# Another order of the work inside a 128-row step of an adaLN cross-attention: DVE, ScalarE and GpSimd queues rearranged

## The reference

```python
def _ada_ln(x, c, W_ss, b_ss):
    h = (x - mu) / jnp.sqrt(var + EPS)
    scale, bias = jnp.split(silu(c) @ W_ss + b_ss, 2, axis=-1)
    return (1.0 + scale)[:, None, :] * h + bias[:, None, :]

xq  = _ada_ln(x_q,  t_vec, Wss_q,  bss_q)       # x_q  (16, 1024, 512)
xkv = _ada_ln(x_kv, t_vec, Wss_kv, bss_kv)      # x_kv (16, 64, 512)
q = (xq @ Wq + bq).reshape(B, Lq, 16, 32)
kv = (xkv @ Wkv + bkv).reshape(B, Lkv, 2, 16, 32)
scores = einsum('bqhd,bkhd->bhqk', q, k) / sqrt(32)
out = einsum('bhqk,bkhd->bqhd', softmax(scores), v).reshape(B, Lq, H)
return x_q + (out @ Wp + bp)
```

## Time and profile before

| what | us |
|---|---|
| median of 3 runs | 1309.93 (1308.97 to 1312.77) |
| the profiled execution's own time | 1311.49 |
| its span, first to last instruction | 1309.7 |
| busy: TensorE | 1165.9 (89%) |
| busy: VectorE | 1050.9 (80%) |
| busy: ScalarE | 872.3 (67%) |
| busy: GpSimd | 841.6 (64%) |

### The profile page before, as it was taken

The page is one execution under the profiler, slowest core; times in us unless marked ns, Lnnn a source line. Parts: engine busy times, 40 slices in busy tenths (PEclk is TensorE's granted clock), DMA queues, the critical chain, the costliest instruction groups (busy, mean ns, idle before and its releaser), DMA issues.

```text
span 1309.7 us, 32556 instructions
## 1 busy us (share of the span) xinstructions
PE 1165.9 (89%) x11072; PEld 693.8 (53%) x11072; DVE 1050.9 (80%) x1799; ACT 872.3 (67%) x1624; POOL 841.6 (64%) x941
## 2 busy tenths in 40 slices
PE   6897799898989998998989999898999999898997
PEld 2673455555555555554555555454555555454554
DVE  5746788888888888787888888787978888888896
ACT  2476667676776676676767677676766667676654
POOL 1544466767666776766666676766667675766744
PEclk9799899999999999999999999999999999999999
DMA  9010122222222222222222222222222222222222
GB/s 331 31 50 17 57 74 89 83 96 72 96 72 96 72 96 72 96 96 72 95 73 96 72 96 72 86 93 77 89 88 82 86 76 92 72 97 74 82 77 78
DMA packets 59871, 112.00 MB, mean 86 GB/s; under 512 B 6412, under 2 KB 6440, under 8 KB 59832
## 3 DMA queue, kind: packets, MB, share of 16 engines
q1 hardware_dynamic: 59832, 111.48, 25.0%
HBM read 77.90 MB, written 33.55 MB: 85 GB/s over the span
## 4 chain that ended last, share of the span: by engine, by line
PE 25%; issue 22%; POOL 18%; DVE 12%; ACT 10%; DMA 1%; POOLq 1%; ACTq 1%; DVEq 0%; SPq 0%
PE ps_q L1133 8%; PE ps_o L1201 7%; POOL xr L394 5%; POOL w_lo L432 4%; POOL xh L385 3%; PE ps_v L1116 3%; PE ps_t L1167 3%; DVE pr L876 3%; ACT junk L583 2%; POOL rstd L373 2%; DVE pr L896 2%; PE ps_s L1152 2%; PE ps_v L1186 2%; ACT xT_hi L510 2%; DVE mx L884 2%
## 5 line engine op out<-in xcount | busy, mean ns | idle before, releaser
L394 POOL TENSOR_TENSOR xr<-xr,bp_row 128x512 f32<-128x512 f32 x128 | 163.0, 1273 | 140.1 <-DMA xr<-in_x_dram 72.1
L603 ACT ACTIVATE pr<-pr,exp_scale 128x1024 f32<-128x1024 f32 x128 | 147.1, 1150 | 123.0 <-DVE pr L896 123.0
L558 ACT CAST pt_hi<-ps_t 128x512 f16<-128x512 f32 x256 | 138.0, 590 | 107.8 <-PE ps_t L1167 107.8
L846 DVE TENSOR_TENSOR xT_lo<-ps_v,xT_hi 128x512 f16<-128x512 f32 x120 | 83.0, 692 | 140.3 <-ACT xT_hi L510 140.3
L418 POOL TENSOR_TENSOR xr<-y,xr 128x512 f32<-128x512 f32 x128 | 162.5, 1270 | 25.5 <-POOL rstd L373 7.3
L425 POOL TENSOR_TENSOR half_den<-pr 128x512 f32<-128x512 f32 x128 | 162.9, 1272 | 22.8 <-DVE den L861 22.8
L432 POOL TENSOR_TENSOR w_lo<-w_tmp,w_hi 128x512 f16<-128x512 f32 x60 | 69.7, 1162 | 167.4 <-ACT w_hi L591 165.4
L884 DVE TENSOR_REDUCE mx<-ps_s 128x8 f32<-128x512 f32 x256 | 164.0, 683 | 12.4 <-PE ps_s L1152 12.4
L876 DVE SCALAR_TENSOR_TENSOR pr<-pr,ps_v 128x512 f32<-128x512 f32 x256 | 164.5, 684 | 4.4
L904 DVE TENSOR_TENSOR pt_lo<-ps_t,pt_hi 128x512 f16<-128x512 f32 x256 | 163.8, 682 | 0.2 <-ACT pt_hi L558 0.2
L896 DVE TENSOR_TENSOR pr<-ps_s,mx 128x512 f32<-128x512 f32 x256 | 163.8, 682 | 0.0
(11 more groups left out here) (162 smaller groups left out, 2348.9 us busy)
## 6 DMA issues: line engine op xcount, KB each, us to landing
x_in<-in_x_dram SPq DMA_DIRECT2D x128, 256.0 KB, 2.7
xr<-in_x_dram SPq DMA_DIRECT2D x128, 256.0 KB, 2.9
out_dram<-xr SPq DMA_DIRECT2D x128, 256.0 KB, 2.0
raw<-in_L_xcond_Wss_kv_dram SPq DMA_DIRECT2D x4, 512.0 KB, 5.4
cx<-in_ctx_dram SPq DMA_DIRECT2D x1, 2048.0 KB, 12.7
raw<-in_L_xcond_Wss_q_dram SPq DMA_DIRECT2D x4, 512.0 KB, 13.7
raw<-in_L_xcond_Wkv_dram SPq DMA_DIRECT2D x2, 1024.0 KB, 15.7
wq<-in_L_xcond_Wq_dram SPq DMA_DIRECT2D x1, 1024.0 KB, 17.0
```

Source lines behind the costliest of these rows:

```text
L394: pool.tensor_tensor(xr[:, s, :], xr[:, s, :], bp_row[:, :], ALU.add).then_inc(xr_ready, 1)
L558: act.copy(pt_hi[:, 4 * h:4 * h + 4, :], ps_t[:, h, :].rearrange("p (g n) -> p g n", g=4))\
L603: act.activation(pr[:, i % 2], pr[:, i % 2], ACT.Exp, scale=exp_scale[:, 0:1]).then_inc(exp_done, 1)
```

## The change

Only the order of calls inside three `step` functions changes, and with it which unit some calls handle. TensorE's and SP's code is untouched. No arithmetic is added or removed; ScalarE's prologue takes in the moments of one more unit (9), since `sum_rows` and `sum_squares` now run one unit further ahead, and `residual` handles unit i-4 where it handled i-2. The preparation of the query weights (`scaled_wq`, `scaled_wq_lo`) is one step later on GpSimd, `scaled_wq_hi` in the same step as before, and `values` moves from step 1 to step 2.

```diff
 # GpSimd
             def step(b, i):
-                half_sums(b, i - 1)
-                if 2 <= i <= 5:
-                    scaled_wq_lo(b + 1, i - 2)
-                if 1 <= i <= 4:
-                    scaled_wq(b + 1, i - 1)
                 await_rows(b, i + 9)
-                residual(b, i - 2)
+                residual(b, i - 4)
                 moments(b, i + 9)
                 await_moments(b, i + 9)
+                half_sums(b, i - 1)
+                normalise(b, i + 9)
                 add_rows(b, i - 4)
-                normalise(b, i + 9)
+                if 3 <= i <= 6:
+                    scaled_wq_lo(b + 1, i - 3)
+                if 2 <= i <= 5:
+                    scaled_wq(b + 1, i - 2)
 # ScalarE
                 turned_p(b, i - 2, 1)
-                sum_rows(b, i + 9)
+                if i == 2:
+                    values(b)
+                sum_rows(b, i + 10)
+                if i == 7:
+                    key_blocks(b + 1)
+                if i == 4:
+                    query_bias(b + 1)
+                query(b, i + 4)
+                turned_x(b, i + 8)
+                sum_squares(b, i + 10)
                 if exists(b, i):
...
                     wait(act, sub_done, 2 * upto(b, i))
                     act.activation(pr[:, i % 2], pr[:, i % 2], ACT.Exp, scale=exp_scale[:, 0:1]).then_inc(exp_done, 1)
-                turned_x(b, i + 8)
-                if i == 4:
-                    query_bias(b + 1)
-                query(b, i + 4)
-                sum_squares(b, i + 9)
+                if 2 <= i <= 5:
+                    scaled_wq_hi(b + 1, i - 2)
                 if isinstance(b, int) and b == 0 and i in (0, 1):
                     wp_high(i)
-                if 2 <= i <= 5:
-                    scaled_wq_hi(b + 1, i - 2)
-                if i == 1:
-                    values(b)
-                if i == 7:
-                    key_blocks(b + 1)
 # ScalarE, prologue
                         row_moments(8)
+                        row_moments(9)
 # VectorE; softmax_shift now takes the half h and does that half alone
             def step(b, i):
-                turned_o(b, i - 3)
                 score_max(b, i, 0)
                 score_max(b, i, 1)
-                softmax_shift(b, i)
+                turned_o(b, i - 3)
+                weight_sums(b, i - 1)
                 turned_p(b, i - 2, 0)
                 turned_p(b, i - 2, 1)
+                denominators(b, i - 1)
+                softmax_shift(b, i, 0)
+                softmax_shift(b, i, 1)
                 turned_x(b, i + 8)
-                weight_sums(b, i - 1)
-                denominators(b, i - 1)
+                query(b, i + 4)
                 if isinstance(b, int) and b == 0 and i in (0, 1):
                     wp_low(i)
                 normalise_p(b, i - 1)
-                query(b, i + 4)
```

More of the change, by code:

```diff
@@ L886, in score_max, with softmax_shift @@
                        .then_inc(mx_done, 1)
-            def softmax_shift(b, off):
+            def softmax_shift(b, off, h):
                 if not exists(b, off):
                     return
[L892 to L898, removed]
+                if h == 0:
+                    wait(dve, p_turned, 2 * unit(b, off - 1))
+                hs = slice(HALF * h, HALF * (h + 1))
+                wait(dve, mx_done, 2 * unit(b, off) + h + 1)
+                dve.tensor_tensor(pr[:, off % 2, hs, :], ps_s[:, h, :].rearrange("p (h l) -> p h l", l=LKV),
+                                  mx[:, hs].unsqueeze(2).to_broadcast([P, HALF, LKV]), ALU.subtract)\
+                   .then_inc(sub_done, 1)
             def turned_p(b, off, h):
```

## The result

The changed kernel takes 1184.82 us in the median of 4 runs (1183.3 to 1185.47), against 1311.06 for the kernel before in its own 4 runs; the ratio is 0.9036, with a 95% interval of 0.9018 to 0.9054. The forecast was 1184. The profiled execution took 1185.47, its span is 1183.7.

A forecast was written before the change was run, and what follows sets the result against it. The kernel was taken to be bound by TensorE's 8.21 us a step plus waits from a ring across engines. Gains of 119.4 + 6.2 = 125.6 us took the span from 1309.7 to 1184.1, the forecast median to 1184; range 1176 to 1226.

The forecast's parts named there:

- TensorE's floor: Steps from unit 8 to unit 120: each falls to TensorE's unwaited 8.21 us, 919.5 in all, a gain of 119.4 us.
- The ring through `w_hi`, `w_lo` and `xh`: ScalarE, GpSimd and TensorE, steps 2 to 5: w_lo's wait for w_hi delays xh; its 4.72 us in step 3 go.
- VectorE in time for `weigh` and the scores: VectorE's step: all five results TensorE wants are ready in time; least slack 0.57 us, xT_lo for weigh.
- The late exponential and `vb`, `kb` for nothing: ScalarE: vb in step 2 and kb in step 7, 1.33 us a pair, fill a wait; later exponential, 1.15, still in time.
- Start: Up to unit 8: first scores some 1.6 us later, unit 3 unchanged within 2 us, then five steps gain 6.2 us.
- The possible gain from a clock that stays up: TensorE's clock around 128 to 130 us: halving the wait could keep it up, some 3 us better, left for the range.
- End: The last eight units: already at their floors, no change taken.
- The half sums can start when the exponential ends, at 7.6: GpSimd: half sums start 0.6 us before the next step's scores and end 0.7 after; den wants them at 2.8.
- (a): TensorE: weigh waits for xT_lo, 0.3 us a step giving 1220 us, 0.6 giving 1256; chance 0.2 with cases between.
- (b): GpSimd's last third binds: w_hi waits for w_tmp if the full step is 8.7 us; 22 us, 1206; chance 0.1.
- (c): Slower: the late exponential closes a ring from turn_x to the next step's weigh; 30 us longer, 1340; chance 0.04.
- (d): The order makes no difference: a wait is for something else and returns at another instruction; 1310 us; chance 0.02.

The follow-up runs named there:

- less_pe: The changed kernel without the product of oT_hi with the low half of the output weights (4 of 12 matrix products of project_out); 1116.97 us, ratio 0.8528.
- w_last: The kernel before with only GpSimd's weight work (w_lo, w_tmp) moved from behind the half sums to the end of its step; 1273.64 us, ratio 0.9707.
- w_same_step: The changed kernel with GpSimd's weight quarters one step earlier, in the steps of the kernel before; 1326.26 us, ratio 1.0119.
- undo_dve: The changed kernel with VectorE's old order; 1226.54 us, ratio 0.9342.
- undo_dve_q: The changed kernel with VectorE's old order, but q_lo ahead of the sums; 1186.78 us, ratio 0.9035.
- exp_early: The changed kernel with ScalarE's exponential back in its early place, ahead of kb, q_hi and xT_hi; 1432.74 us, ratio 1.0909.
- start: The changed kernel with unit 9's row moments behind the last prologue halves on ScalarE, and VectorE normalising ahead of wp_low; 1181.24 us, ratio 0.9006.
- act_only: The kernel before with ScalarE's new order alone (late exponential, moments one unit further ahead); 1375.98 us, ratio 1.0488.
- undo_pool: The changed kernel with GpSimd's old order; 1443.73 us, ratio 1.0993.
- dve_only: The kernel before with VectorE's new order alone; 1772.54 us, ratio 1.351.
- pool_only: The kernel before with GpSimd's new order alone; 1972.43 us, ratio 1.5034.

## Why the prediction was right

The time (1184 against 1184.82) came out by its own steps, and not by errors that cancelled in the large terms: 119.75 us less between units 8 and 120 (119.4 reckoned) and 6.2 between units 3 and 8 (6.2). The small terms cancelled in part by luck, as said at the start below.

- *TensorE's floor.* Every step from unit 3 to unit 120 at 8.21: shown, 919.15 us for 112 steps against 919.5. That it is TensorE which sets it is shown by `less_pe`.
- *The ring through `w_hi`, `w_lo` and `xh`.* The 4.72 us wait is gone. I gave two reasons, that `w_lo` takes the `w_hi` of the step before and that it stands behind `xh`. For the ring of the kernel before the second is enough, as `w_last` shows, which has no wait at `w_lo` left. The first is needed in the new order, where `w_hi` stands behind the late exponential: `w_same_step`, without it, closes another ring.
- *VectorE in time for `weigh` and the scores.* Right; `xT_lo` has 0.82 us of slack where I had 0.57, since the reciprocal starts 0.16 us ahead of the subtraction and not 0.3, and `den` 0.60 ahead of `pt_lo` and not 0.7. `undo_dve` and `undo_dve_q` show that `q_lo` is the deadline that mattered.
- *The late exponential and `vb`, `kb` for nothing.* Right in the new order; `exp_early` shows what the early place costs there.
- *Start.* First scores 1.4 us later (1.6 reckoned), unit 3 at 147.28 against 147.38 before (no change reckoned), then 41.04 us for five steps (41.05 reckoned). The size of the first is right (1.8 us at full clock, by the stretches compared under `start`), but in this execution half clock ahead of the first scores, which I had not reckoned with, would have made them late by itself. Counted from the first product of the values, the first scores are 2.0 us later and unit 3 is 0.6. That the effects before unit 3 cancelled this closely was luck within the 2 us that I allowed; over all the kernels here the three steps from the first scores to unit 3 take 25.1 to 31.5 us. The possible gain from a clock that stays up did not come, as the windows of the changed kernel show (PEclk is the third number from the end):

```profile
125.00:130.00 5.00, 3.16 (x14) 1.09 (x9) 2.99 (x4) 3.94 (x8) 3.77 (x5) 0.58 0.02 3
...
135.00:140.00 5.00, 1.47 (x7) 1.47 (x8) 3.62 (x5) 1.66 (x3) 4.32 (x5) 0.60 0.20 51
```

  Part of either stretch ran at half clock (1.2 GHz); it fell within idle times of TensorE, the first of 1.84 us, where it was 4.21 before, the second of 4.56 us ahead of the first turned weights. The Trainium skill ("TensorE: Matmul & The Clock Gate", What's actually happening) says that idle time closes the gate, and both stretches agree. That halving the wait would keep the clock up was my own inference from it, and the first stretch does not bear it out.
- *End.* 76.23 us from unit 120 on, against 1309.7 - 1233.49 = 76.21.

Three steps of the prediction were off without touching the sum. "The half sums can start when the exponential ends, at 7.6": they start 0.7 us after the scores of the next step (607.56 against 606.86), 1.3 us later than I had them, since the bias row ahead of them waits for the squares; GpSimd's idle time stands ahead of the bias row and not of the half sums. `den` is as close to its deadline as `xT_lo`, 0.8 us. And GpSimd's full step, put at 7.8 us, is 7.9. The rivals: (a) no wait of `weigh` in the steady steps; (b) no wait of `w_hi`; (c) not in this kernel, but I had given rings of that kind too little thought; (d) no. In `act_only` and `undo_pool` I expected to stay below the kernel before and they ended 5 and 10 per cent above it, and `dve_only` was put at 1330 and took 1773; each time I had missed an instruction that merely stood ahead in a queue. The prediction held because in the changed kernel each of these rings is open, not because I had seen them all.

## What to carry to other kernels

Between engines that run fixed queues, read a change of order as a set of deadlines against the bounding engine's floor, and then follow every ring: from an instruction to its reader, up that reader's whole queue, and back. The three orders here hang together: alone each costs 5 to 50 per cent, together they give 9.6, of which ScalarE's and GpSimd's give 6.6 without VectorE's. What keeps the new ring open is one step of distance between a producer at the end of one queue and its reader in the other, which cost no work at all. And where an order makes TensorE wait, look at its granted clock beside the waits: in the slow kernels here its own work took longer, too.

## What the runs showed of the hardware

`wp_low`, a VectorE operation that reads two SBUF operands, and a GpSimd operation that reads SBUF take turns. `wp_low` alone takes 1.21 us (`pool_only`, first line below), GpSimd's `xh` alone 0.77. In `exp_early` `wp_low` starts 0.04 us after the half sums and takes 2.30 us:

```profile
139.27 1.21 DVE L935 SCALAR_TENSOR_TENSOR wp_lo<-xr,scale,wp_hi 128x1024 f16<-128x1024 f32 x1
```

```profile
139.26 2.30 DVE L937 SCALAR_TENSOR_TENSOR wp_lo<-xr,scale,wp_hi 128x1024 f16<-128x1024 f32 x1 [0.40 <-ACT wp_hi L624]
139.22 1.25 POOL L425 TENSOR_TENSOR half_den<-pr 128x512 f32<-128x512 f32 x1
140.46 1.74 POOL L385 TENSOR_SCALAR xh<-x_in,neg_mean,rstd 128x512 f32<-128x512 f32 x1
```

In every run where the half sums are under way when `wp_low` starts, it ends 1.08 us after them, however long it has stood there; the half sums keep their 1.26. An `xh` that starts behind `wp_low` takes 1.73 to 1.83 us and ends 0.56 to 0.65 us after it. The Trainium skill ("SBUF — State Buffer", Who interferes with whom) has the second of the two wait until the first is done, and these times agree, but for a tenth or two at the handover. In the changed kernel this touches two `wp_low` and two `xh`.
